# A four-layer graph kernel: other instructions and another order in its first stage, which normalises x and splits the weights

## The reference

```python
h = jnp.maximum(_layernorm(x, axis=-1), 0.0)      # (x - m) / sqrt(v + 1e-5)
x = x + _L0_gnn_ref(h, adj, adj, Wq, Wk, Wv, Wout)   # 8 heads of attention, bias and mask from adj
h = jnp.maximum(_layernorm(x, axis=-1), 0.0)
x = x + _L1_gnn_ref(h, adj, ...)                  # two steps of nucleus attention and diffusion
...                                               # L2, L3: products with the normalised adj
```

## Time and profile before

| | |
|---|---|
| median of three runs | 3580.87 us |
| the profiled execution | 3579.35 us |
| its span, first to last instruction | 3577.4 us |
| what lies around the span | 1.95 us |
| PE / DVE / ACT busy | 82% / 65% / 36% of the span |
| POOL busy | 1% |
| mean granted TensorE clock | 0.923 of full speed |
| `setup`, until the first load of `adjacency` | 0 to 70.56 us |

### The profile page before, as it was taken

One profiled execution on the slowest core, in us unless ns is written; L12 is line 12 of the kernel. 1 busy time (PEld: TensorE's weight loads), 2 busy tenths in 40 slices (PEclk: granted clock), 3 DMA queues, 4 the chain that ended last, 5 costly groups with the idle time before them and its releaser, 6 DMA issues. The chain is left out here.

```text
span 3577.4 us, 57809 instructions
## 1 busy us (share of the span) xinstructions
PE 2916.8 (82%) x20312; PEld 2138.2 (60%) x20312; DVE 2320.2 (65%) x4566; ACT 1276.1 (36%) x1644; POOL 50.2 (1%) x68
## 2 busy tenths in 40 slices
PE   1469999999999999999999566885677468686599
PEld 1346666767667676676766244664545356575488
DVE  6965556555565555555555599789587988895430
ACT  4643433444333443434433222332213343421211
POOL 0000000000000000000000100000000000000110
PEclk9579999999999999999999788997888789898899
DMA  5946748386583856838477110100011000110500
GB/s 216 374 160 169 184 111 197 97 195 165 130 198 96 200 132 160 202 92 199 118 170 188 50 47 24 60 31 18 1 45 36 1 25 24 36 36 4 218 1 25
DMA packets 586123, 396.75 MB, mean 111 GB/s; under 512 B 538371, under 2 KB 551174, under 8 KB 560390
## 3 DMA queue, kind: packets, MB, share of 16 engines
q1 hardware_dynamic: 584262, 382.49, 39.3%
q10 hardware_dynamic: 1728, 12.58, 1.1%
HBM read 223.05 MB, written 37.75 MB: 73 GB/s over the span
## 5 line engine op out<-in xcount | busy, mean ns | idle before, releaser
L675 DVE SCALAR_TENSOR_TENSOR e_lo<-e,e_hi 128x2048 f16<-128x2048 f32 x128 | 293.2, 2291 | 444.0 <-ACT e_hi L600 444.0
L554 PE MATMUL av<-vw_hi,pT_hi 128*128 128x256 f16 x2048 | 559.7, 273 | 5.9 <-DMA pT_lo<-e_lo 5.9
L554 PE MATMUL av<-vw_hi,pT_lo 128*128 128x256 f16 x2048 | 559.9, 273 | 0.0
L554 PE MATMUL av<-vw_lo,pT_hi 128*128 128x256 f16 x2048 | 559.8, 273 | 0.0
L543 PE MATMUL logits<-kT_hi,qT_hi 128*128 128x512 f16 x1024 | 389.0, 380 | 7.9 <-DVE att_small L661 5.9
L1753 DVE SCALAR_TENSOR_TENSOR nuc_junk<-nuc_e,nuc_thr 128x2048 bf16<-128x2048 f32 x168 | 388.4, 2349 | 4.7
L543 PE MATMUL logits<-kT_lo,qT_hi 128*128 128x512 f16 x1024 | 388.1, 379 | 0.0
L543 PE MATMUL logits<-kT_hi,qT_lo 128*128 128x512 f16 x1024 | 388.1, 379 | 0.0
L594 ACT ACTIVATE att_small<-att_small,minus 128x1 f32<-128x1 f32 x128 | 37.7, 295 | 830.2 <-DVE att_small L670 830.2
L661 DVE CUSTOM_DVE_ANT_0 e<-logits,bias,att_small 128x1024 f32<-128x1024 f32 x256 | 328.6, 1284 | 0.0
L595 ACT ACTIVATE e<-e,att_small,sc 128x2048 f32<-128x2048 f32 x128 | 266.2, 2080 | 0.0
(11 more groups left out here) (394 smaller groups left out, 5777.2 us busy)
## 6 DMA issues: line engine op xcount, KB each, us to landing
bias<-bias_scratch SPq DMA_DIRECT2D x130, 1024.0 KB, 4.8
bias_scratch<-adj_bias SPq DMA_DIRECT2D x16, 1024.0 KB, 8.2
adjT_scratch<-adjT SPq DMA_DIRECT2D x16, 1024.0 KB, 7.6
nuc_at_hi<-adjT_scratch SPq DMA_DIRECT2D x32, 512.0 KB, 3.9
nuc_at_lo<-adjT_scratch SPq DMA_DIRECT2D x32, 512.0 KB, 4.8
adjT<-adjT_scratch SPq DMA_DIRECT2D x16, 1024.0 KB, 20.5
adj_rows<-in_adj_dram ACTq DMA_DIRECT2D x12, 1024.0 KB, 9.3
adj_rows<-in_adj_dram SPq DMA_DIRECT2D x4, 1024.0 KB, 7.9
```

The source lines that it names most:

```text
L554: last = nc.tensor.matmul(AV[par][:, :], PT[par][w][:, m, :], VW[x][:, m, :], start=(m == 0 and w == x == 0), stop=(m == T - 1 and w == 1))
L675: nc.vector.scalar_tensor_tensor(out=EL[:, :], in0=E[par][:, :], scalar=P_SCALE, in1=EH[:, :], op0=ALU.mult, op1=ALU.subtract).then_inc(lo ...
```

## The change

ScalarE normalises and rectifies in one instruction for each tile: relu(rstd * x + minus), with rstd multiplied by 16 beforehand and minus = -mean * rstd, both made by VectorE in one small instruction each. The 16 instructions of VectorE at L237 are gone. Each of the eight transposed blocks has a PSUM bank of its own, and TensorE waits only for its four rectified tiles. ScalarE copies the blocks before it makes the weights' f16 parts, not behind. VectorE takes three remainders behind `extremes`, five behind the scales, and none behind the weights' remainders.

```diff
-        tp = [ps(c, f"h_tp{n}", [P, BANK]) for n in range(2)]
+        tp = [ps(c, f"h_tp{n}", [P, BANK]) for n in range(8)]
...
-                for t in range(T):
-                    nc.vector.tensor_scalar(hx[:, t, :], hx[:, t, :], mv[:, t, 0:1], rstd[:, t:t + 1],
-                                            ALU.subtract, ALU.mult).then_inc(centred, 1)
-                for n in range(4):
+
+                def extreme(n):
                     v.wait_ge(w_loaded[n], 16)
                     w = stage[n][:, :, :] if n < 3 else wo[:, :, :]
                     link.note(nc.vector.tensor_reduce(ext[:, 4 + n:5 + n], w, mybir.AxisListType.XY, ALU.max, apply_absolute_value=True))
+
+                def remainder(b):
+                    k, t0 = b % KC, b // KC * BANK
+                    v.wait_ge(h_hi, b + 1)
+                    nc.vector.tensor_tensor(hT_lo[:, k, t0:t0 + BANK], tp[b][:, :], hT_hi[:, k, t0:t0 + BANK],
+                                            ALU.subtract).then_inc(h_lo, 1)
+
+                v.wait_ge(rstd_done, 1)
+                v.wait_ge(stats_done, 1)
+                link(nc.vector.tensor_scalar(rstd[:, :], rstd[:, :], H_SCALE, None, ALU.mult))
+                nc.vector.scalar_tensor_tensor(out=minus[:, :], in0=mv[:, :, 0], scalar=-1.0, in1=rstd[:, :],
+                                               op0=ALU.mult, op1=ALU.mult).then_inc(aimed, 1)
+                for n in range(4):
+                    extreme(n)
                 link.wait()
                 nc.vector.tensor_scalar(ext[:, 0:4], ext[:, 4:8], 1e-30, None, ALU.max).then_inc(extremes, 1)
+                for b in range(3):
+                    remainder(b)
                 v.wait_ge(largest, 1)
...
                 v.wait_ge(powers, 1)
+                for b in range(3, 8):
+                    remainder(b)
                 for n in range(3):
                     v.wait_ge(w_hi, n + 1)
                     link(nc.vector.scalar_tensor_tensor(out=WL[n][:, :, :], in0=stage[n][:, :, :], scalar=winv[:, n:n + 1],
                                                         in1=WH[n][:, :, :], op0=ALU.mult, op1=ALU.subtract))
-                for b in range(2 * T // 4):
...
             @block.scalar
             def _(s):
+                s.wait_ge(aimed, 1)
                 for t in range(T):
-                    s.wait_ge(centred, t + 1)
-                    nc.scalar.activation(hx[:, t, :], hx[:, t, :], ACT.Relu, scale=H_SCALE).then_inc(rectified, 1)
+                    nc.scalar.activation(hx[:, t, :], hx[:, t, :], ACT.Relu, bias=minus[:, t:t + 1], scale=rstd[:, t:t + 1]).then_inc(rectified, 1)
+                for b in range(2 * T // 4):
+                    k, t0 = b % KC, b // KC * BANK
+                    s.wait_ge(h_tp, b + 1)
+                    nc.scalar.activation(hT_hi[:, k, t0:t0 + BANK], tp[b][:, :], ACT.Copy).then_inc(h_hi, 1)
                 s.wait_ge(powers, 1)
                 for n in range(3):
                     nc.scalar.activation(WH[n][:, :, :], stage[n][:, :, :], ACT.Copy, scale=winv[:, n:n + 1]).then_inc(w_hi, 1)
...
             @block.tensor
             def _(pe):
                 pe.wait_ge(ident_made, 1)
-                pe.wait_ge(rectified, T)
                 for b in range(2 * T // 4):
                     k, t0 = b % KC, b // KC * 4
-                    if b >= 2:
-                        pe.wait_ge(h_lo, b - 1)
+                    pe.wait_ge(rectified, t0 + 4)
```

More of the change, by code:

```diff
@@ L188, in setup @@
     extremes, largest, powers, w_hi, stats_done = sem("extremes"), sem("largest"), sem("powers"), sem("w_hi"), sem("stats_done")
-    rstd_done, centred, rectified, h_tp, h_hi, h_lo = (sem(s) for s in ("rstd_done", "centred", "rectified", "h_tp", "h_hi", "h_lo"))
+    rstd_done, aimed, rectified, h_tp, h_hi, h_lo = (sem(s) for s in ("rstd_done", "aimed", "rectified", "h_tp", "h_hi", "h_lo"))
     ident_made = sem("ident_made")
@@ L194, in setup @@
         stats, mv = sb(c, "stats", [P, T, 6]), sb(c, "mv", [P, T, 2])
-        rstd = sb(c, "rstd", [P, T])
+        rstd, minus = sb(c, "rstd", [P, T]), sb(c, "minus_mean", [P, T])
         ext = sb(c, "ext", [P, 8])
         wo = acc
-        tp = [ps(c, f"h_tp{n}", [P, BANK]) for n in range(2)]
+        tp = [ps(c, f"h_tp{n}", [P, BANK]) for n in range(8)]
         block = nc.Block()
@@ L233, in _ @@
                 nc.vector.memset(ext[:, :], 0.0).then_inc(stats_done, 1)
-                v.wait_ge(rstd_done, 1)
-                v.wait_ge(stats_done, 1)
-                for t in range(T):
-                    nc.vector.tensor_scalar(hx[:, t, :], hx[:, t, :], mv[:, t, 0:1], rstd[:, t:t + 1],
-                                            ALU.subtract, ALU.mult).then_inc(centred, 1)
-                for n in range(4):
+                def extreme(n):
                     v.wait_ge(w_loaded[n], 16)
@@ L260, in _ @@
                                                         in1=WH[n][:, :, :], op0=ALU.mult, op1=ALU.subtract))
+            @block.scalar
+            def _(s):
+                s.wait_ge(aimed, 1)
+                for t in range(T):
+                    nc.scalar.activation(hx[:, t, :], hx[:, t, :], ACT.Relu, bias=minus[:, t:t + 1], scale=rstd[:, t:t + 1]).then_inc(rectified, 1)
                 for b in range(2 * T // 4):
                     k, t0 = b % KC, b // KC * BANK
[L263 to L269, removed]
-                    s.wait_ge(centred, t + 1)
-                    nc.scalar.activation(hx[:, t, :], hx[:, t, :], ACT.Relu, scale=H_SCALE).then_inc(rectified, 1)
+                    s.wait_ge(h_tp, b + 1)
+                    nc.scalar.activation(hT_hi[:, k, t0:t0 + BANK], tp[b][:, :], ACT.Copy).then_inc(h_hi, 1)
                 s.wait_ge(powers, 1)
@@ L274, in _ @@
                     nc.scalar.activation(WH[n][:, :, :], stage[n][:, :, :], ACT.Copy, scale=winv[:, n:n + 1]).then_inc(w_hi, 1)
-                for b in range(2 * T // 4):
-                    k, t0 = b % KC, b // KC * BANK
-                    s.wait_ge(h_tp, b + 1)
-                    nc.scalar.activation(hT_hi[:, k, t0:t0 + BANK], tp[b % 2][:, :], ACT.Copy).then_inc(h_hi, 1)
             @block.tensor
@@ L282, in _ @@
                 pe.wait_ge(ident_made, 1)
-                pe.wait_ge(rectified, T)
                 for b in range(2 * T // 4):
                     k, t0 = b % KC, b // KC * 4
-                    if b >= 2:
-                        pe.wait_ge(h_lo, b - 1)
+                    pe.wait_ge(rectified, t0 + 4)
                     for t in range(4):
-                        last = nc.tensor.transpose(tp[b % 2][:, t * P:(t + 1) * P], hx[:, t0 + t, k * P:(k + 1) * P], ident[:, :])
+                        last = nc.tensor.transpose(tp[b][:, t * P:(t + 1) * P], hx[:, t0 + t, k * P:(k + 1) * P], ident[:, :])
                     last.then_inc(h_tp, 1)
```

## The result

The changed kernel takes 3532.64 us (median, 3530.72 to 3535.14) where the kernel before takes 3581.11 us beside it: 48.5 us less, ratio 0.9865, 95% interval 0.985 to 0.988. The forecast of 3568.6 us and its range of 3563.5 to 3573 are missed. The time is near that of the first rival, the branch taken once less (3528), and 4.6 us above it.

The account below looks back on a forecast made before the run. It took VectorE's queue from 19.45 to 60.6 us, then the ring through two PSUM banks, to bound `setup`; -4.74 + 1.32 + 0.32 - 9.16 = -12.3 us, from 3580.87 to 3568.6 us, range 3563.5 to 3573.

Parts of the forecast that it names:

- the first rival: In the first step of `nucleus`, different rounding of h loses the branch: 40.7 us less, 3528 us; chance 0.05.
- (a): In `setup`, centring leaves VectorE and two small instructions replace it ahead of the maxima: -4.74 us.
- (b): In `setup`, three remainders of h run on VectorE ahead of its wait for `largest`: +1.32 us.
- (c): In `setup`, five remainders of h fill VectorE's idle time ahead of `wq_lo`: +0.32 us.
- (d): At the end of `setup`, nothing stands behind `wv_lo`, which ends the stage: -9.16 us.
- the later phases: Behind `setup`, shifts from TensorE's clock or the earlier start: 2 us to either side, in the range only.
- Everything behind shifted by one constant: Sign in the new timeline: all phases behind `setup` come earlier by the same amount, 12.3 us in the sum.
- TensorE's clock: Granted clock, read as 1.00 in `setup` through 31 us without a matmul; later shifts allowed 2 us either side.
- (e): In `setup`, banks, TensorE and ScalarE's 16 tiles (5.26 us) and copies lie under the maxima, 9.8 us to spare: no cost.
- a gain given back to a wait in `setup`: In `setup`, late ScalarE work or Wout's late landing takes back gain: 3571 to 3577 us; chance 0.05.
- a branch in another group: In `nucleus`, rounding makes a row of group 0, 1 or 3 take the branch: 3609 us; chance 0.03.

Follow-up runs that it names:

- before_no_branch: Kernel before, with the surplus question in `exceeds` asked of 0.999 of the surplus, so the `nucleus` branch is not taken: 3538.28 us, ratio 0.988.
- after_branch: Changed kernel, with the surplus question in `exceeds` asked of 1.0006 times the surplus, so the `nucleus` branch is taken: 3572.84 us, ratio to before 0.9977.
- two_pass_again: Changed kernel with ScalarE in two passes, x - mean, then relu of rstd times that: 3573.38 us, ratio to before 0.9982.

## Why the prediction was wrong, point by point

| term | said | measured |
|---|---|---|
| (a) centring off VectorE | -4.74 | -4.9 (maxima at 19.73, before 24.61) |
| (b) three remainders | +1.32 | +1.1 (`extremes` to `am`) |
| (c) five remainders | +0.32 | +0.3 |
| (d) the end, to the next load | -9.16 | -8.9 (the barrier took 1.04, not 0.82) |
| sum, to the next load | -12.3 | -12.45 |
| the branch | 0 in the sum, chance 0.05 of -40.7 | -42 |
| the later phases | 0, 2 to either side | +6 (of the medians, what the rows above leave) |
| all | -12.3 | -48.5 |

- **The step that failed** is the branch in `nucleus`, put at nothing in the sum, with a chance of only 0.05 that it goes. It went, and was worth 42.1 and 42.6 us by the medians of before against `before_no_branch`. The place and the price (40.7 us) were right, and the reason (rounding) fits all the runs. The evidence against it failed. I had worked out a surplus of three f32 steps for row 372, under my own order of summing, and took it for the chip's. The chip's is at most one step. My exact sum, given with `after_branch`, has the same row 2.8e-4 of its threshold short, some 13 steps to the other side. A margin of three steps in an arithmetic whose order of sums I did not know was none. That the surplus was under 1 part in a million of the row's sum was the finding, and it gave no ground to hold the one outcome likelier than the other. On which side the new form fell was then luck; that the branch's going brings 42 us is not.
- **"Everything behind shifted by one constant"** failed as well. That all engines have the same instructions in the same order behind the barrier was true and not enough: VectorE's stand 14 places earlier, and `nucleus` is 6 us longer. The range had 2 us for TensorE's clock. This term was too small also for its own reason: the stretch behind `nucleus` differs by 4 us between executions of one kernel.
- The bounds of the terms, at their upper ends, add to -11.1 and not -11.2 us. Nothing hangs on it.
- (a) to (d) held within 0.3 us each. In (b) the reduction on GpSimd took its 0.40 us beside running remainders, as it did alone, and `am` followed the third directly. By the Trainium skill, page "SBUF — State Buffer", section "Who interferes with whom", a VectorE instruction with only one input in SBUF does not contend with GpSimd, and the trace agrees.
- (e) had the size of ScalarE's work too small: 16 tiles took 7.98 us, not 5.26. In before ScalarE was fed by VectorE every 0.33 us; with scale and bias both taken for each partition it needs 0.50, and 0.41 in each of the two passes of `two_pass_again`. The copies ended at 31.7 and not at 30, still 7.8 us ahead of `winv`, for which ScalarE then waited. Wout was there in time.
- The rival of a gain given back to a wait in `setup` did not occur; nor did a branch in another group.
- TensorE's clock: the prediction took the 1.00 of before, from 29 to 60 us without a matmul, as measured. In the changed kernel, where the transposes end at 29, the same stretch is:

```profile
29.00:60.00 31.00, 0.00 (x0) 0.00 (x0) 28.15 (x28) 13.58 (x9) 0.40 (x1) 0.58 0.25 76
```

  That is 1.00 until 33 us and 0.50 from 34. By the Trainium skill, page "TensorE: Matmul & The Clock Gate", section "What's actually happening", an idle array stands at half clock, and this row agrees. Before's row is no evidence against it. The transposes tell the pace: all 32 of before, then those of the changed kernel from 20 to 26.8 and from 27 to 30 us:

```profile
L289 PE MATMUL h_tp<-ident,hx x32: 417/421/477, 25.3 to 68.0; 128*128 128x128 f32 x32
```

```profile
L296 PE MATMUL h_tp<-ident,hx x20: 411/421/476, 22.1 to 26.6; 128*128 128x128 f32 x20
```

```profile
L296 PE MATMUL h_tp<-ident,hx x13: 272/273/411, 26.6 to 28.7; 128*128 128x128 f32 x13
```

  The view gives 1.00 for all of them, and also for 0 to 20 us, ahead of any matmul, in both kernels. But in the changed kernel one takes 421 ns until 26.6 us and 273 ns behind that, and in before 421 ns to the last, at 68 us. So before's TensorE most likely stood at the lower level too in these stretches, and the 1.00 there is the value with which the view begins. It cost nothing in the comparison: the distance of 12.4 us holds through `adjacency`.

## What to carry to other kernels

Where a program branches on its data, list the branches, their lengths and how near the data stand to them, before pricing a change that alters the last bit of anything ahead; and compare two kernels with the branch held equal. Read how often the branch's lines ran before asking which edit made the gain: here 42 of 48.5 us belong to a coin that fell the other way, and only 12.45 to the work, of which 6 were lost again. An expected gain that arrives short by a fixed amount, whatever delay is added, may lie in where the instructions stand; a few instructions under a wait test that cheaply. And profile each kernel twice before reading a few microseconds out of one profile: here the stretch behind `nucleus` differed by 4 us between executions of one kernel, while `nucleus`, without the branch, held within 0.1 us.

## What the runs showed of the hardware that was not expected

- 14 or 30 memsets of one column under a wait in the first 20 us shorten a phase that runs from 2032 to 3241 us by 6.2 and 6.6 us; 6 do not (1202.7 and 1202.3 against 1209.2).
- A ScalarE pass over 128x256 with scale and bias from SBUF takes 0.50 us, with one of them 0.41 us.
- The granted clock in the view can be wrong at the start: it reads 1.00 to 79 us in before, where the transposes take 421 ns each; in the changed kernel the same instruction goes from 421 to 273 ns at about 27 us, with the view at 1.00 on both sides.
- The same kernel's last stretch took 290.3 us in one profile and 286.3 in another, with TensorE's granted clock at 0.85 and 0.95 from 3325 to 3360 us.
- One kernel's runs lie up to 10 us apart (before: 3575.26 to 3585.64 in 16 runs), so that 5 us could be told only from several runs of each and from the lengths of phases in the profiles.
